# In-place last normalisation: the result leaves from the residual's tile, and the scratch squares move to the attention tile

## The reference

```python
# first half: gated delta rule, 16 heads of 16
x_act = tanh(x);  static_out = x_act @ W.T
S = lam * S;  u = beta * (v_t - S.T @ k_t);  S = S + outer(k_t, u);  o_t = S.T @ q_t     # per token and head
y = layernorm(static_out + o) * ln_gamma + ln_beta
x1 = layernorm(x + y)
# second half: 256 -> 768 -> 256, weights are int32 / 127
out = layernorm(x1 + (silu(x1 @ wg.T) * (x1 @ wu.T)) @ wd.T)
```

## Time and profile before

| | us |
|---|---|
| median of 3 runs | 1717.36 |
| lowest, highest | 1714.75, 1728.76 |
| the profiled execution, its own time | 1734.76 |
| its span, first to last instruction | 1733.0 |

### The profile page before, as it was taken

One profiled execution on the slowest core, in us unless ns is written; L12 is line 12 of the kernel. 1 busy time (PEld: TensorE's weight loads), 2 busy tenths in 40 slices (PEclk: granted clock), 3 DMA queues, 4 the chain that ended last, 5 costly groups with the idle time before them and its releaser, 6 DMA issues.

```text
span 1733.0 us, 53678 instructions
## 1 busy us (share of the span) xinstructions
PE 1373.0 (79%) x21032; PEld 1070.7 (62%) x21032; DVE 1359.0 (78%) x3461; ACT 1118.9 (65%) x2357; POOL 839.5 (48%) x1106
## 2 busy tenths in 40 slices
PE   4358778888887888878888888888888878888765
PEld 3346666666666666666666666666666666666532
DVE  4578888888888788888888888888888888888731
ACT  3336667666766767666776666766766666776543
POOL 6024455445444545444455554444555444455542
PEclk9558989888988999888999998989998898898866
DMA  4555544555554555555555665654555655555200
GB/s 119 116 106 119 111 114 114 117 118 111 130 111 116 113 123 117 117 119 118 116 121 118 118 121 112 124 116 114 123 120 108 115 119 117 116 120 109 57 13 25
DMA packets 701325, 190.98 MB, mean 110 GB/s; under 512 B 620944, under 2 KB 688528, under 8 KB 701072
## 3 DMA queue, kind: packets, MB, share of 16 engines
q1 hardware_dynamic: 701072, 187.56, 50.3%
HBM read 103.55 MB, written 67.11 MB: 98 GB/s over the span
## 4 chain that ended last, share of the span: by engine, by line
DVE 24%; SPq 22%; DMA 16%; PE 15%; issue 11%; ACT 8%; POOL 3%; ACTq 0%; POOLq 0%; DVEq 0%
SPq L1060 9%; DMA scr_g<-gs 6%; DMA xa<-L_attn_x 6%; PE pg L253 4%; SPq L1073 4%; PE pc L182 4%; DVE tt L451 4%; PE pu L253 4%; SPq L995 3%; DVE gs L443 3%; DVE gate L495 2%; DVE xt L406 2%; DVE x1lo L488 2%; DMA y_out<-v 2%; DVE U L382 2%
## 5 line engine op out<-in xcount | busy, mean ns | idle before, releaser
L954 POOL TENSOR_TENSOR hlo<-gate,hhi 128x512 f16<-128x512 f32 x192 | 263.7, 1383 | 377.3 <-ACT hhi L784 375.4
L182 PE MATMUL pc<-R,tb 128*128 128x32 f16 x4096 | 158.2, 186 | 128.1 <-DVE R L372 125.2
L182 PEld LDWEIGHTS pc<-R,tb 128*128 128x128 f16 x4096 | 146.7, 118 | 148.9 <-DVE R L372 145.7
L182 PE MATMUL pc<-U,kb 128*128 128x32 f16 x4096 | 158.9, 188 | 95.4 <-DVE U L382 95.3
L182 PEld LDWEIGHTS pc<-U,kb 128*128 128x128 f16 x4096 | 146.9, 118 | 124.7 <-DVE U L382 124.6
L182 PEld LDWEIGHTS pc<-S,e 128*128 128x128 f16 x4096 | 151.9, 118 | 61.7 <-DVE S L399 55.9
L182 PE MATMUL pc<-S,e 128*128 128x32 f16 x4096 | 157.3, 186 | 38.8 <-DVE S L399 38.7
L279 PE MATMUL pd<-wd_t,hhi 128*128 128x256 f16 x768 | 178.2, 278 | 7.9 <-POOL hlo L954 5.6
L279 PE MATMUL pd<-wd_t,hlo 128*128 128x256 f16 x768 | 178.0, 278 | 0.0
L216 PEld LDWEIGHTS pf<-xb,e 128*128 128x128 f16 x4096 | 153.6, 118 | 32.9 <-DMA e<-scr_x 17.6
L216 PE MATMUL pf<-xb,e 128*128 128x32 f16 x4096 | 156.2, 191 | 18.5 <-DMA e<-scr_x 16.9
(11 more groups left out here) (134 smaller groups left out, 3229.0 us busy)
## 6 DMA issues: line engine op xcount, KB each, us to landing
xa<-L_attn_x SPq DMA_DIRECT2D x128, 128.0 KB
scr_x<-xt SPq DMA_DIRECT2D x64, 256.0 KB, 2.1
xb<-scr_x SPq DMA_DIRECT2D x256, 64.0 KB, 2.8
e<-scr_x SPq DMA_DIRECT2D x256, 64.0 KB, 3.5
scr_g<-gs SPq DMA_DIRECT2D x32, 512.0 KB, 3.5
gh<-scr_g SPq DMA_DIRECT2D x32, 512.0 KB, 3.4
kb<-k SPq DMA_DIRECT2D x512, 32.0 KB, 2.2
scr_t<-t SPq DMA_DIRECT2D x64, 256.0 KB, 3.5
```

What stands on the lines that cost most here:

```text
L182: last = pe.matmul(pc2[:, :, cols], stationary(h, a), moving[:, :, cols], start=a == 0, stop=a == 1)
L954: pool.tensor_tensor(hlo[:, t, :], gate[:, t % 2, :], hhi[:, t, :], ALU.subtract).then_inc(SEM["hl"], 1)
```

## The change

The last norm writes `x1` in place, and the store reads that tile. The squares of the first variance, which are never read, go to the piece's own dead half of `v` instead of the `x1` tile. The waits follow the tiles. No instruction is added or removed, and none changes its place in any list.

```diff
 act_static_out (writes v[:, p])
             if g == 0:
                 act.wait_ge(SEM["res"], n_of("res", q - 2))
-                act.wait_ge(SEM["out"], n_of("out", q - 3))
+                act.wait_ge(SEM["va3"], n_of("va3", q - 3))
+            act.wait_ge(SEM["va2"], n_of("va2", q - 2, 2 * g + 2))
 act_variance
-            x_, to, nq, va = ((res, x1_of(q), nq2, va2), (x1_of(q), v[:, 1 - p], nq3, va3))[z - 2]
+            x_, to, nq, va = ((res, v[:, p], nq2, va2), (x1_of(q), v[:, 1 - p], nq3, va3))[z - 2]
...
-                elif z == 2:
-                    act.wait_ge(SEM["o"], n_of("o", q - 1))
-                elif q == NS - 1:
-                    act.wait_ge(SEM["out"], n_of("out", q - 2))
-                else:
+                elif z == 3 and q < NS - 1:
                     act.wait_ge(SEM["res"], n_of("res", q + 1))
 act_first_norm (writes x1)
             if n == 0:
                 act.wait_ge(SEM["nm2"], n_of("nm2", q))
+                if q < NS - 1:
+                    act.wait_ge(SEM["out"], n_of("out", q - 1))
 act_last_norm
-            act.activation(v[:, 1 - p, n, :], x1_of(q)[:, n, :], ACT.Identity, bias=nm3[:, n:n + 1],
+            act.activation(x1_of(q)[:, n, :], x1_of(q)[:, n, :], ACT.Identity, bias=nm3[:, n:n + 1],
 sp_store_out
-                sp.dma_start(out[...], v[:, 1 - p, n, :]).then_inc(SEM["out"], 16)
+                sp.dma_start(out[...], x1_of(q)[:, n, :]).then_inc(SEM["out"], 16)
```

More of the change, by code:

```diff
@@ L1090, in sp_store_out @@
                     sp.wait_ge(SEM["out"], n_of("out", q - 1))
-                sp.dma_start(out[:, q * T + n * C:q * T + (n + 1) * C, :], v[:, 1 - p, n, :]).then_inc(SEM["out"], 16)
+                sp.dma_start(out[:, q * T + n * C:q * T + (n + 1) * C, :], x1_of(q)[:, n, :]).then_inc(SEM["out"], 16)
         def sp_step(sp, s, p):
```

## The result

| | before | after |
|---|---|---|
| median of 12 runs each, us | 1717.63 (1712.70 to 1728.76) | 1707.05 (1699.24 to 1710.84) |
| ratio | | 0.9931, 95% interval 0.9911 to 0.9952 |
| the profiled execution, its own time | 1734.76 | 1699.24 |

The new kernel is faster by 0.7%, 12 us, between 8 and 15. Timed once more beside the old kernel, the same kernel (`e_after`) had 0.9936, 0.9913 to 0.9958, which is 11 us, between 7 and 15. The forecast of 1714 us had the sign and the place of the gain, and its range of 1705 to 1729 held the time, 2 us from the lower end. The gain that it foresaw, 3.5 us, is about a third of the measured one.

A forecast was written before the change was run, and what follows sets the result against it. The prediction took a loop through all engines, one turn per 50 us step, to bound the kernel. Its terms, -4.5 for the store's wait and +1.0 for added waits, gave -3.5 us: 1717.36 to 1714 us, range 1705 to 1729.

The forecast's parts named there:

- What bounds the kernel: No engine is full; a loop through all engines, one turn per 50 us step, with line 706 on it in most steps.
- The store's wait leaves line 706: At line 706, 7 stalls for stores to land vanish and the saving reaches SyncE: -4.5 us, ends 0 and -4.5.
- The same wait at the first norm: Moved to line 758, the wait is met early, 1.2 us to spare in the tightest step found: 0 us.
- The waits for ScalarE's own squares: At line 706 and elsewhere, 59 more waits, mostly hidden: +1.0 us, between 0 and 4.7.
- The tiles: Last norm in place and squares into another tile keep their durations, about 590 and 497 ns: 0 us.
- The larger gain by the tanh's waits: Earlier line 406 starts SyncE's turn sooner; half of the tanh's 30.7 us waits for `x` go: 1698 us, chance 0.06.
- The stalled first norm: At line 757, late stores stall ScalarE in 30 steps; 2.4 us later landing costs 18 us: 1735 us, chance 0.07.
- the eaten gain: All 59 added waits exposed, +4.7 against -4.5, or hardly any stall in timed runs: 1717 to 1718 us, chance 0.27.
- The sum: Whole kernel: -4.5 + 1.0 = -3.5 us, taken from the median 1717.36 to give 1714 us.
- The chances: Whole kernel: 0.05 faster by more than 1%, 0.89 within 1%, 0.06 slower; a gain of 2 to 4.5 us had 0.60.

The follow-up runs named there:

- e_x_sooner: New kernel with SyncE issuing the load of `x` behind five of the eight `tb` loads instead of all eight: 1695.81 us, ratio to before 0.9835.
- e_wait_back: New kernel with the store's wait also back at the first instruction of the static product: 1719.69 us, ratio to before 0.9979.
- e_waits_only: Old kernel with the new kernel's added waits on top, nothing taken away: 1722.38 us, ratio to before 0.9995.
- e_wait_back2: New kernel with the store's wait back at the static product, timed again on another chip: 1726.61 us, ratio to before 1.0010.

## Why the prediction was right, and what it mis-sized

*What bounds the kernel.* Right: the loop through SyncE's queue, the tanh's wait for `x` and line 706. `e_x_sooner` shows it, since relieving that loop by a reordering on SyncE gave 28 us against the old kernel, 17 of them beyond the change. That line 706 lay on it in nearly every step is shown by its start 0.10 us behind the landing in 26 of 29. What the prediction left out is the recurrence's line 668 right behind line 706, the second path.

*The store's wait leaves line 706, -4.5 us.* Right in place and kind: putting it back returns the kernel to 0.9979 and 1.0010. The prediction read line 706 as free to start at 1298.97, the end of the accumulator read; in the traces of after it starts 0.10 us ahead of that end. Mis-sized, and this is the term that made the forecast small. I called -4.5 the most that there could be, "no more idle time of that kind exists". The table of waits lists idle time above 0.15 us, and ScalarE has none when it merely loses the overlap of 0.10 us with the instruction before. Measured against that overlap the same trace holds 7.4 us, where the tables gave 4.5 and 5.2. The rows that would have said so were there: line 706's first instruction in an ordinary step, with any other pair of the same timeline beside it, where line 752 begins 0.09 before the end of line 673.

*The same wait at the first norm, 0.* Right: no wait of line 757 for `y_out` in either trace. The 1.2 us to spare were reckoned too small. In that step line 706, which waited for the same four stores, stands in ScalarE's timeline as

```profile
851.65 1.09 ACT L706 ACTIVATE v<-pf 128x512 f32<-128x512 f32 x2
```

so the stores had landed by then, 2.7 us ahead of the first norm at 854.31, and not at 853.1.

*The waits for ScalarE's own squares, +1.0 us.* Too dear. Alone they are 0.9995 (0.9977 to 1.0013), and the overlap at line 707 is whole. By the figure of the Trainium skill, "Advanced Engine Details and Errata", miscellaneous facts, that reading a semaphore takes 50 to 100 ns, an estimate would have put 3 to 6 us here. The 0.04 + 0.04 us of the earlier trace rows, for a wait that is late, are of that size, and so are the 0.18 us instead of 0.10 from landing to start in `e_wait_back`; the traces of after show that met waits disappear behind the running instruction.

*The tiles, 0.* Right as far as is known: 591 and 496 ns, and 0.9995 as the mean of the two runs with the new tiles and the old wait, which leaves up to some 5 us open.

*The larger gain by the tanh's waits, 6 in 100.* The time did not go there: 28.9 us after at the median, 30.7 and 26.0 before. Its first half did happen, since SyncE waited 12 to 19 us less for the transposed keys than in the trace before. *The stalled first norm* did not come, *the eaten gain* neither.

*The sum.* The wait, by the ratios of the kernels without and with it, 0.9934 and 0.9995 as means of two, is worth 0.0061 or 10.5 us, of which about 2 are the further waits of `e_wait_back`. By the gaps it is 7.4 and 7.3 us in the two traces of the old kernel, and the first trace, from which I worked, was not an unlucky one. Measured are 12 and 11 us (8 to 15 and 7 to 15). The some 4 us between are not accounted for: the scatter of the gaps from one execution to the next is as large, the tiles are not excluded, and neither is the granted clock, which was 0.872 in the mean of the old kernel's runs and 0.874 in those of `e_after`, a difference that goes with less than 1 us among the runs of either kernel.

*The chances.* "Within 1%" had 0.89, and that is what came. The gain of 2 to 4.5 us, which had 0.60, is not; what came lies between that case and the larger gain, where no case of the prediction stood. The range held it because its lower end had been taken down from 1710 to 1705 for a part of the larger gain, by a mechanism that did not act. In that the hit is in part luck.

## What to carry to other kernels

Judge a wait by where its releaser arrives in all repetitions, not by the cases that the table of waits lists: compare the start of the waiting instruction with the overlap that its engine shows elsewhere, and a wait that is met "just in time" in most steps shows as a lost 0.1 us in each. When such a wait is found, a little of the engine's own list may be all that has to lie between: here half a microsecond, the second static product, did as well as the first norm. And ask why the releaser is late. Moving three transfers behind the load of `x` was worth 17 us on the new kernel, more than the change itself, and with them moved the change was worth 0.0016 instead of 0.0069 and 0.0064, though the intervals overlap.

## What the runs showed of the hardware

Waits on a semaphore that are already met cost nothing behind a running ScalarE instruction: four ahead of line 707, and the instruction begins 0.10 us before its predecessor's end. A wait that is met late delays its instruction by a fixed time after the last landing: 0.10 us with three waits at the place, in 26 of 29 steps of both traces of the old kernel, 0.15 us with five in `e_waits_only`, and 0.18 us with five in another order in `e_wait_back` and `e_wait_back2`. The last norm takes 591 ns when it writes over its own input and 590 into another tile. And the same kernel's profiled executions may differ by 10 us (1697.4 and 1708.0 us of span), with the tanh's waits for `x` at 18.7 and 28.9 us: one trace is not enough to say where a gain of 0.7% came from.
